# Three bf16 planes in place of fp32 for the sums by node of a graph network's second layer

## What is computed

```python
h = jnp.maximum(_layernorm(x, axis=-1), 0.0)
# _L1_gnn_ref(h, edge_index, edge_feat, ...):
edge = jnp.concatenate([h[source], h[target], edge_feat], axis=-1)   # 48 + 48 + 16 values per edge
h1 = jax.nn.relu(edge @ W1 + b1)                                     # 128
h2 = jax.nn.relu(h1 @ W2 + b2)                                       # 128
message = h2 @ W3 + b3                                               # 48
msum = jax.ops.segment_sum(message, target, num_segments=n)
cnt = jax.ops.segment_sum(ones, target, num_segments=n)
x = x + (h + msum / jnp.maximum(cnt, 1.0)[:, None])
```

## Time and profile before

| | us |
|---|---|
| median of 3 runs | 7833.55 |
| lowest, highest | 7828.76, 7835.27 |
| the profiled execution | 7827.43 |
| its span | 7825.6 |

### The profile page before, as it was taken

One profiled execution on the slowest core, in us unless ns is written; L12 is line 12 of the kernel. 1 busy time (PEld: TensorE's weight loads), 2 busy tenths in 40 slices (PEclk: granted clock), 3 DMA queues, 4 the chain that ended last, 5 costly groups with the idle time before them and its releaser, 6 DMA issues. The chain is left out here.

```text
span 7825.6 us, 170502 instructions
## 1 busy us (share of the span) xinstructions
PE 6391.6 (82%) x51894; PEld 5150.0 (66%) x51895; DVE 3453.2 (44%) x8798; ACT 1910.4 (24%) x3646; POOL 3518.3 (45%) x3525
## 2 busy tenths in 40 slices
PE   3758999999998868888888888888788887888788
PEld 3646887888777646666666666666666666666666
DVE  9989888888784622222222222222222222222222
ACT  1216555555451411111111111111111111111111
POOL 4550000000110355655555556555556555655555
PEclk9999999999999567777778877878777877787777
DMA  6015777777676333333333333333333333333333
GB/s 140 0 36 217 253 248 240 249 251 250 232 236 216 88 96 87 86 88 86 86 87 87 87 86 86 88 86 88 87 86 88 86 88 87 86 87 86 87 87 67
DMA packets 556931, 959.03 MB, mean 123 GB/s; under 512 B 277229, under 2 KB 356303, under 8 KB 556455
## 3 DMA queue, kind: packets, MB, share of 16 engines
q1 hardware_dynamic: 401687, 644.10, 26.3%
q0 software_dynamic: 155136, 313.54, 15.4%
HBM read 682.14 MB, written 275.03 MB: 122 GB/s over the span
## 5 line engine op out<-in xcount | busy, mean ns | idle before, releaser
L1333 POOL DMA_INDIRECT p_got<-p_tab,idx_d x3136 | 2975.4, 949 | 2007.5 <-remote 944.8
L1319 ACT ACTIVATE h<-z,b_col 128x512 f32<-128x512 f32 x784 | 538.7, 687 | 4034.2 <-remote 2819.4
L1323 DVE TENSOR_TENSOR h<-z,nb 128x512 f32<-128x512 f32 x784 | 538.8, 687 | 2196.1 <-remote 1521.9
L1305 PE MATMUL z<-w_sb,h 128*128 128x128 f32 x6272 | 1127.4, 315 | 433.8 <-issue 398.9
L1305 PEld LDWEIGHTS z<-w_sb,h 128*128 128x128 f32 x6272 | 1054.6, 229 | 547.0 <-issue 488.1
L790 PE MATMUL a_ps<-tile_r,pair_l 128*128 128x288 bf16 x6272 | 1229.6, 292 | 182.4 <-DVE tile_r L841 76.5
L808 PE MATMUL out_ps<-gw,a_got 121*128 121x144 bf16 x14256 | 1295.0, 227 | 33.8 <-DVE big L855 21.7
L841 DVE TENSOR_SCALAR tile_r<-iota_r,key_r,dst_i 128x576 bf16<-128x576 f16 x3136 | 1173.9, 432 | 280.3 <-PE a_ps L790 130.0
L770 ACT CAST stage<-a_ps 128x576 uint16<-128x576 f32 x1568 | 998.8, 638 | 910.8 <-PE a_ps L790 729.8
L1312 PE MATMUL seg_ps<-hot_d,h 128*128 128x32 f32 x6272 | 955.5, 290 | 320.0 <-issue 316.2
L1299 PEld LDWEIGHTS z<-ident_b,p_got 128*128 128x128 bf16 x9408 | 773.6, 118 | 654.8 <-issue 642.0
(11 more groups left out here) (164 smaller groups left out, 3590.9 us busy)
## 6 DMA issues: line engine op xcount, KB each, us to landing
a_got<-a_tab SPq DMA_DIRECT2D x396, 576.0 KB, 3.9
a_tab<-stage SPq DMA_DIRECT2D x392, 576.0 KB
rel<-rel_row SPq DMA_DIRECT2D x392, 192.0 KB
p_got<-p_tab,idx_d POOLq DMA_INDIRECT x3136
ef<-in_edge_t SPq DMA_DIRECT2D x392, 64.0 KB
q_win<-q_tab SPq DMA_DIRECT2D x784, 24.0 KB
a_tab<-big SPq DMA_DIRECT2D x22, 567.0 KB
p_tab<-pq_out SPq DMA_DIRECT2D x14, 672.0 KB, 3.6
```

The source lines that it names most:

```text
L1305: last = pe.matmul(z2[:, j, :], h1_tile, w2_sb[:, :], start=True, stop=True)
L1319: return act.activation(h1[:, :], z1[:, :], ACT.Relu, bias=b1_col[:, 0:1])
L1323: return dve.tensor_tensor(h2[:, :, :], z2[:, :, :], nb2[:, :].unsqueeze(1).to_broadcast([P, GROUP, H]), ALU.max)
L1333: pool.indirect_dma_start(p_rows[:, j, :], None, p_tab, bass.IndirectOffsetOnAxis(idx[:, j:j + 1], 0)).then_inc(landed, 16)
```

## The change

h2 is kept as three bf16 planes whose sum it is, and the sums by node are made with bf16 matmuls. ScalarE copies h2 (fp32) to bf16, `h2_high`. VectorE subtracts that from h2 in place. ScalarE copies the rest to bf16, `h2_mid`, and VectorE subtracts again, into bf16 `h2_low`. TensorE then makes three bf16 matmuls per tile (12 per group) in place of one fp32 matmul per tile (4 per group, 8 instruction pairs), all with the same one-hot, which is now written as bf16 directly. So the cast `hot_c` goes. `h2_high` has 4 buffers, `h2_mid` and `h2_low` have one each; `hot` has 8. The sum by node of a group is now made three steps behind its z1 and added four steps behind, in place of two and two. `q_x`, used only in a rarely run side path, moves into another tile's space.

```diff
+        def sum_planes(pe, seg_ps, planes, hot):
+            nodes = hot.shape[2]
+            for j in range(GROUP):
+                for m, plane in enumerate(planes):
+                    pe.matmul(seg_ps[:, 0:nodes], plane[:, j, :], hot[:, j, :], start=(j == 0 and m == 0),
+                              stop=(j == GROUP - 1 and m == PLANES - 1))
+            for j in range(GROUP):
+                last = pe.matmul(seg_ps[0:1, nodes:2 * nodes], ones_b[:, :], hot[:, j, :], start=(j == 0),
+                                 stop=(j == GROUP - 1))
+            return last
...
-            hot = [sb(f"hot_d{s}", [P, GROUP, SPAN], F32, life) for s in range(UNROLL)]
-            hot_c = [sb(f"hot_c{s}", [P, GROUP, SPAN], BF16, life) for s in range(UNROLL)]
+            hot = [sb(f"hot_d{s}", [P, GROUP, SPAN], BF16, life) for s in range(DEPTH)]
+            h2_high = [sb(f"h2_high{s}", [P, GROUP, H], BF16, life) for s in range(UNROLL)]
+            h2_mid = sb("h2_mid", [P, GROUP, H], BF16, life)
+            h2_low = sb("h2_low", [P, GROUP, H], BF16, life)
...
                 @block.scalar
+                    def keep_high(q, s):
+                        act.wait_ge(h2_ready, q + 1)
+                        wait_past(act, seg_made, q - (UNROLL - 1))
+                        act.copy(h2_high[s % UNROLL][:, :, :], h2[s % 2][:, :, :]).then_inc(high_made, 1)
+                    def keep_mid(q, s):
+                        act.wait_ge(rest_left, q + 1)
+                        wait_past(act, seg_made, q)
+                        act.copy(h2_mid[:, :, :], h2[s % 2][:, :, :]).then_inc(mid_made, 1)
                     def step(q, s):
-                        act.wait_ge(hot_ready, q + 1)
-                        wait_past(act, seg_made, q - (UNROLL - 1))
-                        act.copy(hot_c[s % UNROLL][:, :, :], hot[s % UNROLL][:, :, :]).then_inc(hot_c_ready, 1)
...
+                        if live(q, 2):
+                            keep_mid(q - 2, s)
+                        if live(q, 1):
+                            keep_high(q - 1, (s - 1) % DEPTH)
...
                 @block.tensor
                     def segment(q, s):
-                        pe.wait_ge(h2_ready, q + 1)
+                        pe.wait_ge(low_made, q + 1)
                         pe.sem_inc(pe_turns, 1)
-                        pe.wait_ge(hot_c_ready, q + 1)
+                        pe.wait_ge(hot_ready, q + 1)
                         wait_past(pe, seg_added, q - 1)
-                        sum_by_node(pe, seg_ps[s % 2], h2[s % 2], hot[s % UNROLL], hot_c[s % UNROLL]).then_inc(seg_made, 1)
+                        planes = (h2_high[s % UNROLL], h2_mid, h2_low)
+                        sum_planes(pe, seg_ps[s % 2], planes, hot[s]).then_inc(seg_made, 1)
                     def step(q, s):
-                        if past(q, 2):
-                            segment(q - 2, (s - 2) % UNROLL)
+                        if live(q, 3):
+                            segment(q - 3, (s - 3) % DEPTH)
...
                 @block.vector
                     def keep_h2(q, k):
-                        wait_past(dve, seg_made, q - 1)
+                        wait_past(dve, low_made, q - 1)
+                    def leave_rest(q, s):
+                        dve.wait_ge(high_made, q + 1)
+                        dve.tensor_tensor(h2[s % 2][:, :, :], h2[s % 2][:, :, :], h2_high[s % UNROLL][:, :, :], ALU.subtract
+                                          ).then_inc(rest_left, 1)
+                    def keep_low(q, s):
+                        dve.wait_ge(mid_made, q + 1)
+                        wait_past(dve, seg_made, q)
+                        dve.tensor_tensor(h2_low[:, :, :], h2[s % 2][:, :, :], h2_mid[:, :, :], ALU.subtract
+                                          ).then_inc(low_made, 1)
                     def step(q, s):
                         if not isinstance(q, int) or q + 1 < NG:
                             hots(q + 1, (s + 1) % DEPTH)
-                        if past(q, 1):
+                        if live(q, 3):
+                            keep_low(q - 3, (s - 3) % DEPTH)
+                        if live(q, 2):
+                            leave_rest(q - 2, (s - 2) % DEPTH)
+                        if live(q, 1):
                             keep_h2(q - 1, (s - 1) % 2)
-                        if past(q, 2):
-                            add_segment(q - 2, s % 2)
+                        if live(q, 4):
+                            add_segment(q - 4, s % 2)
```

More of the change, by code:

```diff
@@ L1374, in build_gnn @@
                 hot_ready = sem("hot_ready_d", ctx)
-                hot_c_ready = sem("hot_c_ready", ctx)
+                high_made = sem("high_made", ctx)
+                rest_left = sem("rest_left", ctx)
+                mid_made = sem("mid_made", ctx)
+                low_made = sem("low_made", ctx)
                 hot_t_ready = sem("hot_t_ready_d", ctx)
@@ L1384, in build_gnn, with live @@
                 block = ctx.enter_context(nc.Block())
-                def past(q, back):
-                    return not isinstance(q, int) or q >= back
+                def live(q, back=0):
+                    return not isinstance(q, int) or back <= q < NG + back
                 def slot_count(q, s, per):
@@ L1439, in _ @@
                 def _(act):
[L1440 to L1448 removed]
+                    def keep_high(q, s):
[6 more added lines that the diff above has]
+                        act.copy(h2_mid[:, :, :], h2[s % 2][:, :, :]).then_inc(mid_made, 1)
+                    def step(q, s):
+                        if live(q):
+                            act.wait_ge(z1_made, q + 1)
+                            wait_past(act, z2_made, q - 1)
+                            make_h1(act, h1[s % 2], z1[s % 2]).then_inc(h1_ready, 1)
+                        if live(q, 2):
+                            keep_mid(q - 2, s)
+                        if live(q, 1):
+                            keep_high(q - 1, (s - 1) % DEPTH)
                     paced(act, NG, step, DEPTH)
+                    step(NG, 0)
+                    step(NG + 1, 1)
                 @block.tensor
@@ L1475, in segment @@
                     def segment(q, s):
-                        pe.wait_ge(h2_ready, q + 1)
+                        pe.wait_ge(low_made, q + 1)
                         pe.sem_inc(pe_turns, 1)
-                        pe.wait_ge(hot_c_ready, q + 1)
+                        pe.wait_ge(hot_ready, q + 1)
                         wait_past(pe, seg_added, q - 1)
-                        sum_by_node(pe, seg_ps[s % 2], h2[s % 2], hot[s % UNROLL], hot_c[s % UNROLL]).then_inc(seg_made, 1)
+                        planes = (h2_high[s % UNROLL], h2_mid, h2_low)
+                        sum_planes(pe, seg_ps[s % 2], planes, hot[s]).then_inc(seg_made, 1)
                     def step(q, s):
-                        first(q, s)
-                        if past(q, 1):
+                        if live(q):
+                            first(q, s)
+                        if live(q, 1):
                             second(q - 1, (s - 1) % 2)
-                        if past(q, 2):
-                            segment(q - 2, (s - 2) % UNROLL)
+                        if live(q, 3):
+                            segment(q - 3, (s - 3) % DEPTH)
                     paced(pe, NG, step, DEPTH)
-                    second(NG - 1, (NG - 1) % 2)
-                    segment(NG - 2, (NG - 2) % UNROLL)
-                    segment(NG - 1, (NG - 1) % UNROLL)
+                    for t in range(3):
+                        step(NG + t, t)
                 @block.vector
@@ L1528, in step @@
                             hots(q + 1, (s + 1) % DEPTH)
-                        if past(q, 1):
+                        if live(q, 3):
+                            keep_low(q - 3, (s - 3) % DEPTH)
+                        if live(q, 2):
+                            leave_rest(q - 2, (s - 2) % DEPTH)
+                        if live(q, 1):
                             keep_h2(q - 1, (s - 1) % 2)
-                        if past(q, 2):
-                            add_segment(q - 2, s % 2)
+                        if live(q, 4):
+                            add_segment(q - 4, s % 2)
                     paced(dve, NG, step, DEPTH)
-                    keep_h2(NG - 1, (NG - 1) % 2)
-                    add_segment(NG - 2, (NG - 2) % 2)
-                    add_segment(NG - 1, (NG - 1) % 2)
+                    for t in range(4):
+                        step(NG + t, t)
             with ExitStack() as ctx:
```

9 lines of the change are left out of this document (3 added, 6 removed).

## The result

| | before | after |
|---|---|---|
| device time, median of 4 runs each | 7834.23 us (7828.76 to 7835.27) | 7925.36 us (7919.85 to 7927.52) |
| profiled execution, span | 7825.6 us | 7921.6 us |
| mean granted clock | 0.840 | 0.821 |

The change makes the kernel 1.2% slower: the ratio is 1.0118, 95% interval 1.0102 to 1.0134. The sign is the forecast's, the size a third of it: +91 us where +271 was said (8105 us; the forecast's own range, 7900 to 8350, holds the 7925 at its low end).

A forecast was written before the change was run, and what follows sets the result against it. Bound: a loop in which signals stand still while SyncE issues loads. Profiled 7827.4 us + 265 (held chain) + 5 (end) = 8098; that execution being 6 below the median, 8105 us. Own range 7900 to 8350; 8 in 10: 7650 to 8400.

The forecast's parts named there:

- Rival 1: The copy-subtraction chain keeps up with TensorE, so savings count where TensorE runs freely: 7655 us, with all 7480; chance 0.32.
- (a): TensorE's sums by node: 8 fp32 instruction pairs per group go, 0.98 us at full clock, 1.75 at half.
- (b): TensorE's sums by node: 12 bf16 pairs with 32 moving columns come, 0.5 us per group taken.
- Rival 4: TensorE's bf16 pair costs as much as the fp32 pair, so 12 take 1.37 us: 8195 us; chance 0.02.
- (c): ScalarE loses the one-hot cast (292 ns) and gets two 128x512 copies per group, 0.6 us each taken.
- (d): VectorE gets two 128x512 subtractions per group, 0.6 us each; its load goes from 1.5 to 2.7 us.
- (e): One-hots become bf16 and stay in 8 buffers; transfers and SyncE's queue stay the same: no cost.
- (f): End of the stage: one more turn, with the last group's h2, copies and subtractions in a row: 5 us.
- (g): Added waits around single-buffered h2_mid and h2_low: edge matmuls 0.9 us later in 3/4 of 392 pairs, 265 us.
- The clock: More TensorE stops put more groups at 1.2 GHz; 80 more such groups would add 130 us, giving 8230.
- Rival 2: TensorE's cheaper sums and the chain, caught in fewer pairs, cancel: 7820 to 7850 us; chance 0.08.
- Rival 3: Signals' own path stands still longer with twelve signals a group instead of nine: 243 us more, 8350; chance 0.10.

The follow-up runs named there:

- the run with the fixed place: Kernel before with q_tab's 96 rows read from a fixed place, so SyncE loads no base: 7812.95 us beside 7833.11.
- the small copies: Kernel before with 13 one-element copies added on ScalarE behind each h1, for which nobody waits: 7903.13 us beside 7833.11.

## Why the prediction was right in sign and wrong in size

**What bounds the kernel.** Half right. The pace is a loop with held signals in it, and TensorE's work doesn't set it: the sums' products were a saving of 0.5 us a group that brought nothing, though TensorE worked 576 us less in the stage. Even with the chain loosened (two buffers) the time is the kernel before's to 3 us. Rival 1 had wanted 175 us from that, so it was wrong in more than its condition. But SyncE's issues don't set its length, and GpSimd's rows of gathers belong to it. "GpSimd isn't the bound", 10.0 of 12.7 us, left out that it also stands still at the end of a row until a held signal comes. In the kernel after 268 of 271 pauses (3500 to 7000) are eight gathers apart, and the eight at 1.063 us, the seven gaps between them at 0.325 and the pause of 2.18 are the 12.96 us of the loop. That its 949 ns would stay was an unsaid assumption, and in free groups, of which the trace of before showed nothing, it is the step that would have failed, with 619 us.

**(a), (b)** right. 12 matmuls start from 5010.97 to 5011.25, one each 0.025 us, and the last takes 0.18: 0.46 us for 0.5 taken. Rival 4 is refuted by that.

**(c), (d)** right in size: 618 and 613 ns for the copies, 683 and 680 for the subtractions, 0.6 said for each. ScalarE is busy for 27% of the stage, VectorE for 40%. What was missed is what the subtractions do beside their own time, above.

**(e), (f)** nothing of them shows; the loop's 98 us are already the 96 by which the span grew, to 2.

**(g), the chain**, right in that the wait arises, where it does and by what, and shown by the run with two buffers, which takes it away. As a term of the sum it was wrong: it was to add 0.9 us in three of four pairs, 265 us in all. The edge matmuls do start 1.28 us later behind E (2.66 for 1.38), and in each pair, which alone would be 1.28 x 392 = 502 us; the loop grew by 0.25. "The third let off" was one pair of four in a short window; it stood for nothing.

**The clock** was put in the range and not in the sum. The part from the edge matmuls to z1 takes 0.45 us longer, since it nearly always runs at the 1.2 GHz level behind the stop (edge part 2.08 us at 5006.89, and 1.12 us, the 2.4 GHz level, at 5011.54; the stage's mean fell from 0.79 to 0.77). Over 392 pairs that is 176 us, where the prediction's estimate was 130, though all of that is made up for elsewhere in the loop. The Trainium skill, TensorE: Matmul & The Clock Gate, section "A second HAM failure mode", tells of short idle stretches that make the clock fall and rise again, and the trace agrees that it does so here.

**What failed is the step under the sum,** that the loop hangs on the end of SyncE's issues, E: that signals stand still while SyncE issues, that E stays where it was, and that what comes later behind E therefore lengthens the loop. E came at 6.64 us for 8.12: 0.93 of the 1.48 because SyncE's first issue followed z1 at once (0.30 us for 1.23), 0.55 because the issues themselves took less. The prediction named a change of E as a sign of being wrong, but took it for a term of the time, and it isn't one. One can book 502 + 176 - 580 = 98 us, but these are legs of one measured loop, and the run with the fixed place shows that they don't act by themselves: there E came 3.4 us earlier, the edge matmuls followed 3.4 us later behind it, and the time fell by 20 us. What the runs show in place of E is the end of GpSimd's row of gathers, behind which held signals come through. That the time came out at the low end of the forecast's range is luck: the range was made for delays behind E.

How the single buffers turn into 0.25 us a pair through GpSimd's rows is argued, not shown. With every engine stopped at the same point of each pair, GpSimd stands still after each eight gathers; with two buffers, at 1128 ns a gather, its rows are often of 12 to 24 gathers, and it makes only 151 pauses from 3500 to 7000 for 271. The longer gathers brought no cost that shows there: that kernel has the longest and is no slower than the kernel before.

**Rival 2** (cancelling, 7820 to 7850) was nearer in size than the forecast, but wanted the chain caught in fewer pairs, and it is caught in all. **Rival 3** (more signals hold longer) is against the issues, which got shorter; the small copies' 70 us spoke for something of its kind, and the runs with two buffers and with spare subtractions against it.

**Open:** why a row of gathers holds signals in one group and not in another, in which GpSimd never pauses at all and they still come through; so why the same kernel is free at one time and held at another; the 70 us of the small copies, and the 47 of h2 in PSUM. None of the kernels was clearly faster than the kernel before; two spare subtractions at 0.3% in one run is no version.

## What to carry to other kernels

Where a kernel's pace is a loop of several engines, a new wait's price is what it adds to the loop, less what the stop lets others do sooner: take each leg of the loop from the trace, over all of its turns, and say which legs could move. Legs add up by themselves; whether one of them is the pace only an edit tells that shortens it alone, as the fixed place did here. Give a handover between two engines a second buffer before judging the work it carries: here two buffers took back the 1.2%, in one run (in the kernel with h2 in PSUM, half of it). And before VectorE gets an operation with both operands in SBUF, ask how close GpSimd's gathers are to the pace; one operand left in PSUM removed 9% where GpSimd set the pace.

## What was not expected of the hardware

- Two fp32 subtractions of 128x512 per group with both operands in SBUF lengthen a gather from 951 to 1151 ns on average: 1.60 us with one beside it for over 0.3 us, 0.945 with none. With one operand in PSUM they don't. Spare subtractions on one tile lengthen it to 1000 ns only (free group).
- The same kernel on the same chip takes 6650 or 7830 us, 18% apart, stable to 0.3% within a group of runs, with SyncE's issues for a pair in 3.7 or 6.9 us on average. In the held kind ScalarE's long waits end 1.0 to 2.1 us behind a row of gathers (96% of 400). Without the gathers the times are 5707 and 5874, so nearly all of the difference needs them.
- Weights of 128 bf16 columns with 32 moving columns go at one matmul each 25 ns; as fp32 it was 0.98 us for 8.
